# A recurrent network on one core: GpSimd's order in the steps with the key unit's squares

## The chip, the core and the metric

The kernel runs on one core of a Trainium2 chip. The metric is the device time of one execution in microseconds (us); less is better. Five engines work in parallel, each through its own list of instructions in order: TensorE (PE, matrix products; PEld is its loading of weights), VectorE (DVE), ScalarE (ACT), GpSimd (POOL) and SyncE (SP, which issues transfers). They wait for one another by semaphores.

## The reference

Two levels, each with an attention or state part and a feed-forward part, and at the end a gated sum. The input is 8 sequences of 512 tokens with 128 features. The change touches the last part only, a network of 6 layers:

```
x = level0(x)                       # linear attention, product-key memory
s = mixer_and_experts(norm(x))
for i in range(6):                  # the network
    x = attention(shift(x), Wqkv[i], q_scale[i], k_scale[i], Wo[i]) + x
    x = feed_forward(shift(x), ...) + x
out = x1 + s * silu(x)
```

Attention has 16 heads of 64. Queries and keys are divided by their norm (the root of the sum of their squares over the head), scaled and rotated; each token looks at itself and the 32 tokens before it; the softmax of the scores is taken and multiplied with the values.

## The kernel before

Levels 0 and 1 run first, up to about 2000 us, and are not touched. The network then runs as one software pipeline (function `network`). A **turn** is one layer of one sequence; 6 layers times 8 sequences make 48 turns. Most of them stand in a loop over layers (`Fori` in `turns`), the last ones behind it; one turn flows into the next without a barrier. A turn has 20 **steps**, numbered n. n divides into a group g = n // 5 of four heads and a window t = n % 5 of the tokens (the first of 128 queries, the others of 96, against 128 keys). The order of each engine is written out by hand: each has its own function `step(n, ...)`, and the order in which it calls its helpers is the order of its queue.

What runs in step n:

- PE: transposes the probabilities of step n-2 (`turn_probs`, L508, into the PSUM buffer c_S), scores of step n (`scores`, L493 adds the mask, L498 the products), values of step n-2 (`values`, L522).
- DVE: copies the transposed probabilities of step n-2 (`pt_copy`, L711), the reciprocal of the softmax sums of step n-1 (`inv_sum`, L704, writes c_rs), the row maxima of step n (`row_max`, L695).
- ACT: the output of step n-2 (`out_copy`, L396), the exponentials of step n (`exp`, L385, writes the probabilities c_Pb).
- POOL: the normalisation of the probabilities of step n-1, a product with c_rs (`normalise`, L323).

Beside this, in each group, one **query unit** and one **key unit** of a later group are prepared: two projections into the PSUM buffers c_PA and c_PB (L467 to L469), the squares of both (`square`, L363, on ACT, writes c_sq), their sum c_sqs (`add_squares`, L329, on POOL), the sum over the head (`sumsq`, L474, on PE), logarithm and exponential for the inverse norm (`inverse_norm`, L368 and L370, on ACT), the products with the tables of the rotation (`products`, L674, on DVE, write c_tAB), their sum c_rot (`rotate`, L335, on POOL) and the end (`finish`, L685, on DVE), from which SP copies the unit to its place. The key unit's sum of squares, `sumsq` and rotation stand in the steps with t = 1 (n = 1, 6, 11, 16), the query unit's in those with t = 3 and t = 4.

In a step with t = 1 PE goes through: `turn_probs`, `scores`, `values`, `sumsq` of the key unit, a projection for the values into c_PA (L479 to L481), and in some of them an output or feed-forward product. ACT, behind `exp` of the step, takes L368 and L370 and then copies that projection out of c_PA (`v_copy`, L374). What PE next writes into c_PA waits for this copy: a projection at the start of steps 2 and 17 (L479), the variance of the feed-forward part in step 7 (L541), the next query unit in step 12. `finish_turn` (L741, on DVE, in step 17) writes the new layer input.

Of the kernel before, what the change touches and what calls it, by code (L numbers as in the profile page):

```python
# [98 lines left out]
def network(nc, xf, wh_dram, wt_dram, tab_dram, const, depth, seqs):  # L99
# [8 lines left out]
    with ExitStack() as ctx:  # L108
# [104 lines left out]
        def query(t):  # L213
            return (0, TILE) if t == 0 else (LOOK + t * SPAN_Q, SPAN_Q)
# [4 lines left out]
        def job_k(g, now, nxt):  # L219
            return 2 * ((g + 1) % GROUPS) + 1, now if g < 3 else nxt  # L220

        def job_q(g, now, nxt):
            return 2 * ((g + 2) % GROUPS), now if g < 2 else nxt

        def back(n, d, now, prev):

            return (n - d, now) if n >= d else (n - d + NS, prev)
# [3 lines left out]
        def turns(eng, step):  # L231

            def one(now, nxt, prev, new=None, fresh=False):
                for n in range(NS):
                    step(n, now, nxt, prev, new, fresh)

            def at(l, s):
                return Turn(l, s, seqs)

            for n in range(12, NS):  # L240
                step(n, None, at(0, 0), None, None, False)
            one(at(0, 0), at(0, 1), None)
            with eng.Fori(0, depth - 1) as l:
                for s in range(1, seqs - 1):
                    one(at(l, s), at(l, s + 1), at(l, s - 1))
                one(at(l, seqs - 1), at(l + 1, 0), at(l, seqs - 2), new=l + 1)
                one(at(l + 1, 0), at(l + 1, 1), at(l, seqs - 1), fresh=True)
            l = depth - 1
            for s in range(1, seqs):
                one(at(l, s), at(l, s + 1) if s + 1 < seqs else None, at(l, s - 1))  # L250
            for n in range(18):
                step(n, None, None, at(l, seqs - 1), None, False)

        with nc.Block() as block:
# [59 lines left out]
            @block.gpsimd  # L314
            def _(pool):
                nc.gpsimd.memset(x1s[:, 0:1], 0.0).then_inc(*zeroed.up())

                def normalise(n, turn):
                    pool.wait_ge(*rs_ready.nth(n + 1, turn))
                    m = query(n % TIMES)[1]  # L320
                    p = Pb[0:m, n % 3]
                    r = rs[0:m, n % 2, :].unsqueeze(2).broadcast_to([m, 4, SPAN_K])
                    nc.gpsimd.tensor_tensor(p, p, r, ALU.mult).then_inc(*p_ready.up())  # L323

                def add_squares(j, turn):
                    pool.wait_ge(*squared.nth(2 * j + 2, turn))
                    if j or not turn.first:
                        pool.wait_ge(*summed.nth(j, turn))
                    nc.gpsimd.tensor_tensor(sqs[:, :], sq[:, 0], sq[:, 1], ALU.add).then_inc(*added.up())  # L329

                def rotate(j, turn):
                    pool.wait_ge(*prods.nth(2 * j + 2, turn))
                    if j or not turn.first:
                        pool.wait_ge(*finished.nth(j, turn))
                    nc.gpsimd.tensor_tensor(rot[:, :, :], tAB[:, 0], tAB[:, 1], ALU.add).then_inc(*rotated.up())  # L335

                def step(n, now, nxt, prev, new, fresh):
                    g, t = divmod(n, TIMES)
                    jk, tk = job_k(g, now, nxt)
                    jq, tq = job_q(g, now, nxt)  # L340
                    m, tm = back(n, 1, now, prev)
                    if t == 1 and tk:
                        add_squares(jk, tk)
                    if tm:
                        normalise(m, tm)
                    if t == 1 and tk:
                        rotate(jk, tk)
                    if t == 3 and tq:
                        add_squares(jq, tq)
                    if t == 4 and tq:  # L350
                        rotate(jq, tq)

                turns(pool, step)

            @block.scalar
# [1531 lines left out]
```

## Time and profile before

| what | before |
|---|---|
| median of three runs | 6846.82 us (6841.19 to 6852.91) |
| the profiled execution: time, span of its trace | 6850.26 us, 6848.5 us |
| PE busy | 5618.6 us (82% of the span) |
| DVE busy | 4308.3 us (63%) |
| ACT busy | 3758.7 us (55%) |
| POOL busy | 2607.8 us (38%) |
| the two GpSimd operations that change places | L323: 960 times, mean 1037 ns; L329: 384 times, mean 1268 ns |

The span is that of the trace of one execution. A busy share is a mean over stages with different limits; where time is lost is read in the timeline: a row gives the start, the length, the engine, the source line and the operation, and in brackets how long the engine had been idle and whose work released it. The network fills the span from about 2000 us to its end.

### The profile page before, as it was taken

Reading aid. Unit: us, or ns where it says so; the run is one execution under the profiler, and the core shown is the slowest. Engines: PE = TensorE matmul, PEld = TensorE weight load, DVE = VectorE, ACT = ScalarE, POOL = GpSimd, SP = SyncE. Lnnn points to the kernel's source line nnn. Section 1 sums busy time; section 2 is a strip of 40 time slices with the busy share of each in tenths; the row PEclk is TensorE's granted clock in tenths of the full one; section 3 lists DMA queues with packets and bytes.
Section 4 is the critical chain, followed back from the end, with each engine's and each line's share of the span. In section 5 each row is a group of like instructions: output and inputs, shape, how many; then the busy total and the mean of one; then the engine's idle time right before and its main releaser. Section 6 shows DMA issues by size and latency. Waiting matters only on the chain. (4 is left out here: it accounts for less than half of the span.)

```text
span 6848.5 us, 104092 instructions
## 1 busy us (share of the span) xinstructions
PE 5618.6 (82%) x31008; PEld 3140.3 (46%) x31008; DVE 4308.3 (63%) x6894; ACT 3758.7 (55%) x11846; POOL 2607.8 (38%) x2011
## 2 busy tenths in 40 slices
PE   6777767677768888888888888888888888888887
PEld 2333333222225555555555555555555555555553
DVE  5677766333346666766676666766667666766664
ACT  3444333233226666666666666666666666666665
POOL 1122211000015454444444445454544444454452
PEclk9888888777769999999999999999999999999998
DMA  0000000000012112211122111211122111221112
GB/s 35 0 0 0 0 0 0 19 0 0 0 59 47 44 44 49 51 46 42 43 53 50 42 44 44 54 47 44 44 49 52 44 43 43 53 50 43 42 43 62
DMA packets 160223, 244.35 MB, mean 36 GB/s; under 512 B 51280, under 2 KB 51280, under 8 KB 158928
## 3 DMA queue, kind: packets, MB, share of 16 engines
q1 hardware_dynamic: 159696, 238.08, 14.2%
q8 instruction: 239, 3.92, 0.3%
q14 instruction: 288, 2.36, 0.1%
HBM read 30.26 MB, written 6.29 MB: 5 GB/s over the span
## 5 line engine op out<-in xcount | busy, mean ns | idle before, releaser
L323 POOL TENSOR_TENSOR c_Pb<-c_Pb,c_rs 96x512 f32<-96x512 f32 (+1 forms) x960 | 995.8, 1037 | 1593.7 <-DVE c_rs L704 1590.0
L385 ACT ACTIVATE c_Pb<-c_S,c_nb 96x128 f32<-96x128 f32 (+1 forms) x3840 | 1347.5, 360 | 107.3 <-DVE c_nb L695 102.2
L711 DVE COPY c_PTs<-c_S 128x384 f32<-128x384 f32 (+1 forms) x960 | 559.3, 583 | 953.6 <-PE c_S L508 951.2
L396 ACT ACTIVATE c_OT<-c_PO 128x192 f32<-128x192 f32 (+1 forms) x960 | 327.6, 341 | 1462.8 <-PE c_PO L522 1459.9
L335 POOL TENSOR_TENSOR c_rot<-c_tAB 128x1024 f32<-128x1024 f32 x384 | 909.9, 2369 | 1.2 <-DVE c_tAB L674 0.8
L695 DVE TENSOR_REDUCE c_nb<-c_S 96x4 f32<-96x512 f32 (+1 forms) x960 | 656.7, 684 | 381.8 <-PE c_S L498 373.4
L329 POOL TENSOR_TENSOR c_sqs<-c_sq 128x512 f32<-128x512 f32 x384 | 487.1, 1268 | 847.6 <-ACT c_sq L363 841.9
L385 ACT ACTIVATION_READ_ACCUMULATOR c_Pb<-c_S,c_nb 96x1 f32 (+1 forms) x3840 | 761.2, 198 | 0.0
L498 PE MATMUL c_S<-c_QK 64*96 64x128 f32 (+1 forms) x7680 | 683.9, 298 | 0.0
L508 PEld LDWEIGHTS c_S<-c,c_Pb 96*128 96x128 f32 (+1 forms) x3840 | 441.8, 141 | 445.9 <-issue 418.4
L493 PE MATMUL c_S<-c 128*96 128x256 bf16 (+1 forms) x1920 | 397.8, 290 | 252.0 <-DVE c_PTs L711 247.9
L522 PE MATMUL c_PO<-c_PTs,c_V 128*64 128x96 f32 (+1 forms) x7680 | 568.5, 271 | 1.3 <-DVE c_PTs L711 1.3
L498 PEld LDWEIGHTS c_S<-c_QK 64*96 64x96 f32 (+1 forms) x7680 | 475.7, 170 | 190.7 <-issue 190.7
L508 PE MATMUL c_S<-c,c_Pb 96*128 96x96 f32 (+1 forms) x3840 | 497.8, 251 | 9.1 <-issue 9.1
L979 POOL TENSOR_TENSOR a_AT<-a_AT,c 128x256 f32<-128x256 f32 x128 | 112.6, 880 | 903.7 <-ACT a_AT L1037 903.4
L522 PEld LDWEIGHTS c_PO<-c_PTs,c_V 128*64 128x64 f32 x7680 | 371.6, 140 | 142.4 <-issue 13.5
L493 PEld LDWEIGHTS c_S<-c 128*96 128x96 bf16 (+1 forms) x1920 | 177.7, 120 | 531.4 <-DVE c_PTs L711 442.1
L1122 PE MATMUL a_B<-a_AT,a_V 128*32 128x512 f32 (+3 forms) x1024 | 332.0, 472 | 80.8 <-POOL a_AT L980 80.8
L532 PE MATMUL c_PC<-c_OT,c_WT 128*128 128x512 f32 x768 | 386.6, 606 | 0.0
L685 DVE SCALAR_TENSOR_TENSOR c_F<-c_PA,c_rot 128x1024 f32<-128x1024 f32 x192 | 232.6, 1211 | 71.7 <-ACT c_PA L370 67.4
L467 PE MATMUL c_PA<-c_xh,c_WH 128*128 128x512 f32 x384 | 195.5, 509 | 96.6 <-DVE c_F L685 67.2
L363 ACT ACTIVATE c_sq<-c_PB 128x512 f32<-128x512 f32 x384 | 227.2, 592 | 72.3 <-PE c_PB L469 70.3
(264 smaller groups left out, 10760.1 us busy)
## 6 DMA issues: line engine op xcount, KB each, us to landing
c_QK<-c_F SPq DMA_DIRECT2D x3072, 64.0 KB, 2.0
c_stage<-in_w_heads SPq DMA_DIRECT2D x36, 256.0 KB, 3.0
c_WT<-in_w_tails SPq DMA_DIRECT2D x6, 537.5 KB, 4.5
b_W<-in_w_level SPq DMA_DIRECT2D x1, 3133.0 KB, 10.3
a_W<-in_w_level SPq DMA_DIRECT2D x1, 3078.0 KB, 10.4
c_WT<-in_w_tails SPq DMA_DIRECT2D x6, 512.0 KB, 3.7
x<-in_x SPq DMA_DIRECT2D x1, 2048.0 KB, 7.7
x_kept<-x SPq DMA_DIRECT2D x1, 2048.0 KB, 6.3
```

Of the source, the lines that this page charges most:

```text
L323: nc.gpsimd.tensor_tensor(p, p, r, ALU.mult).then_inc(*p_ready.up())
L329: nc.gpsimd.tensor_tensor(sqs[:, :], sq[:, 0], sq[:, 1], ALU.add).then_inc(*added.up())
L335: nc.gpsimd.tensor_tensor(rot[:, :, :], tAB[:, 0], tAB[:, 1], ALU.add).then_inc(*rotated.up())
L385: e = nc.scalar.activation(Pb[0:m, n % 3, i, :], S[0:m, 2 * (n % 2) + r, c * SPAN_K:(c + 1) * SPAN_K], ACT.Exp, bias=nb[0:m, n % 2, i:i + ...
L493: nc.tensor.matmul(S[0:m, 2 * (n % 2) + r, 0:2 * SPAN_K], const.identb[:, 0:m], const.mask[t > 0], start=True, stop=False, skip_group_chec ...
L498: mm = nc.tensor.matmul(S[0:m, 2 * (n % 2) + r, c * SPAN_K:(c + 1) * SPAN_K], QK[rows, g % 2, 0, c, q0:q0 + m], QK[rows, g % 2, 1, c, k0:k ...
L508: mm = nc.tensor.transpose(S[:, 2 * (n % 2) + r, to:to + m], Pb[0:m, n % 3, 2 * r + c, :], ident[0:m, 0:m])
L522: mm = nc.tensor.matmul(PO[64 * r:64 * r + 64, c * TILE:c * TILE + m], V[:, t, h * DH:(h + 1) * DH], PTs[:, n % 2, 2 * r + c, 0:m], start= ...
L532: nc.tensor.matmul(PC[:, :], WT[:, T_O + p * P:T_O + (p + 1) * P], OT[:, p, :], start=p == 0, stop=p == PAIRS - 1, skip_group_check=True). ...
L695: nc.vector.tensor_reduce(nb[0:m, n % 2].rearrange("p (b c) -> p b c", b=2), S[0:m, b:b + 2, 0:2 * SPAN_K].rearrange("p b (c k) -> p b c k ...
L711: nc.vector.tensor_copy(PTs[:, n % 2].rearrange("p (b c) q -> p b c q", b=2)[:, :, :, 0:m], S[:, b:b + 2, 2 * SPAN_K:].rearrange("p b (c q ...
L1122: mm = nc.tensor.matmul(B[32 * j:32 * j + 32, 6 + g % 2, i * TILE:SEQ], V[:, i, h, :], AT[:, h % 2, SPAN[i]:SPAN[i] + SEQ - i * TILE], sta ...
```

## The change

In GpSimd's `step`, `normalise` now stands ahead of the key unit's `add_squares`. The query unit's half of the function stays. Semaphores, instructions and the other engines' orders are the same.

```diff
                     m, tm = back(n, 1, now, prev)
+                    if tm:
+                        normalise(m, tm)
                     if t == 1 and tk:
                         add_squares(jk, tk)
-                    if tm:
-                        normalise(m, tm)
                     if t == 1 and tk:
                         rotate(jk, tk)
```

GpSimd's queue over a part of a turn, before; the second to fourth rows are one step with t = 1; c_sqs is the sum of squares, c_Pb the probabilities, c_rot the rotated unit:

```order
L323 TENSOR_TENSOR c_Pb<-c_Pb,c_rs 96x512
L329 TENSOR_TENSOR c_sqs<-c_sq 128x512
L323 TENSOR_TENSOR c_Pb<-c_Pb,c_rs 128x512
L335 TENSOR_TENSOR c_rot<-c_tAB 128x1024
L323 TENSOR_TENSOR c_Pb<-c_Pb,c_rs 96x512 x2
```

The same part now:

```order
L323 TENSOR_TENSOR c_Pb<-c_Pb,c_rs 96x512
L323 TENSOR_TENSOR c_Pb<-c_Pb,c_rs 128x512
L329 TENSOR_TENSOR c_sqs<-c_sq 128x512
L335 TENSOR_TENSOR c_rot<-c_tAB 128x1024
L323 TENSOR_TENSOR c_Pb<-c_Pb,c_rs 96x512 x2
```

The normalisation of the window with 128 queries has moved ahead of the key unit's sum of squares; the rotation behind both keeps its place, as do the normalisations behind it.

PE's queue at such a step, before and now: it takes the sum of squares (L474), the projection for the values (L479 to L481), and only then the transposes of the probabilities (L508):

```order
L474 MATMUL c_PB<-c_sqs,c 128x512
L479 MATMUL c_PA<-c_WH,c_xh 128x512
L480 MATMUL c_PA<-c_WL,c_xh 128x512
L481 MATMUL c_PA<-c_WH,c_xl 128x512
L508 MATMUL c_S<-c,c_Pb 128x128 x4
```

Nothing moves on PE, so both of GpSimd's results are asked for in the order sum of squares, then probabilities.

## Rows read from the trace of the kernel before

**Rows 1.** The waits of PE from 2100 to 6800 us: us in total, times, longest us.
```profile
PE c_S L493 <- DVE c_PTs L711: 242.6, 349, 2.7
PE c_PA L541 <- ACT c_V L374: 72.0, 47, 1.6
PE c_PA L479 <- ACT c_V L374: 59.2, 94, 1.6
```

**Rows 2.** One source line, L474: times that PE waited for GpSimd's sum.
```profile
  POOL c_sqs L329: 11.2, 10
```

**Rows 3.** One source line, L323: who waited for the normalised probabilities.
```profile
  PEld c_S L508: 0.4, 1
```

**Rows 4.** The timeline of step 1 of a turn; start us, us, engine, line, [idle before].
```profile
4516.83 1.28 POOL L329 TENSOR_TENSOR c_sqs<-c_sq 128x512 f32<-128x512 f32 x1 [3.13 <-ACT c_sq L363]
4516.85 0.17 DVE L704 RECIPROCAL c_rs<-c_sums 128x4 f32<-128x4 f32 x1
4518.06 1.04 POOL L323 TENSOR_TENSOR c_Pb<-c_Pb,c_rs 128x512 f32<-128x512 f32 x1
4518.42 1.13 PE L474 MATMUL c_PB<-c_sqs,c 128*128 128x512 f32 x2
4520.17 0.68 ACT L368 ACTIVATE c_lnr<-c_PB,c 128x512 f32<-128x512 f32 x1
4520.94 0.60 PE L508 MATMUL c_S<-c,c_Pb 128*128 128x128 f32 x4
4522.14 0.50 PE L479 MATMUL c_PA<-c_WH,c_xh 128*128 128x512 f32 x1 [0.60 <-ACT c_V L374]
```

**Rows 5.** The timeline early in the network, where PE waited for GpSimd's sum.
```profile
2032.72 1.26 POOL L329 TENSOR_TENSOR c_sqs<-c_sq 128x512 f32<-128x512 f32 x1 [6.44 <-ACT c_sq L363]
2034.04 1.12 PE L474 MATMUL c_PB<-c_sqs,c 128*128 128x512 f32 x2 [2.17 <-POOL c_sqs L329]
```

**Rows 6.** The timeline of step 6 of the same turn.
```profile
4542.15 1.13 PE L474 MATMUL c_PB<-c_sqs,c 128*128 128x512 f32 x2
4545.95 1.12 PE L541 MATMUL c_PA<-c_csq,c 128*128 128x512 f32 x2 [1.53 <-ACT c_V L374]
```

**Rows 7.** The timeline of step 11 and the start of step 12.
```profile
4564.12 0.17 DVE L704 RECIPROCAL c_rs<-c_sums 128x4 f32<-128x4 f32 x1
4565.70 1.13 PE L474 MATMUL c_PB<-c_sqs,c 128*128 128x512 f32 x2
4567.99 0.69 DVE L711 COPY c_PTs<-c_S 128x512 f32<-128x512 f32 x1 [1.97 <-PE c_S L508]
4568.74 0.42 PE L493 MATMUL c_S<-c 128*96 128x256 bf16 x2 [0.78 <-DVE c_PTs L711]
```

**Rows 8.** The timeline of step 16 and of step 17 behind it.
```profile
4592.52 0.17 DVE L704 RECIPROCAL c_rs<-c_sums 128x4 f32<-128x4 f32 x1
4594.10 1.12 PE L474 MATMUL c_PB<-c_sqs,c 128*128 128x512 f32 x2
4597.25 0.69 DVE L711 COPY c_PTs<-c_S 128x512 f32<-128x512 f32 x1 [2.83 <-PE c_S L508]
4597.86 0.16 DVE L704 RECIPROCAL c_rs<-c_sums 96x4 f32<-96x4 f32 x1
4597.94 1.50 DVE L741 SCALAR_TENSOR_TENSOR xf<-c_PC,c_WT,c_x1s 64x512 f32<-64x512 f32 x2
4598.10 1.04 POOL L323 TENSOR_TENSOR c_Pb<-c_Pb,c_rs 96x512 f32<-96x512 f32 x1 [1.80 <-DVE c_rs L704]
4599.48 0.69 DVE L690 COPY c_V<-c_PA 128x512 f32<-128x512 f32 x1
4600.09 0.68 DVE L695 TENSOR_REDUCE c_nb<-c_S 96x4 f32<-96x512 f32 x1
```

**Rows 9.** PE's longest wait in the turn, just at the low-clock stretch.
```profile
4579.21 0.79 PE L479 MATMUL c_PB<-c_WH,c_xh 128*128 128x512 f32 x1 [2.07 <-DVE c_tAB L674]
```

**Rows 10.** A window: us, busy us of each engine, PEclk, DMA share, GB/s.
```profile
4578.50:4585.20 6.70, 5.99 (x24) 3.61 (x25) 3.24 (x6) 2.71 (x15) 4.17 (x3) 0.50 0.00 0
```

## The prediction

> **What bounds the kernel now.** I read the page first, for the shares: PE is busy for 82% of the span, no engine for all of it, so the time is set by chains between engines, and what the change is worth must be read at the places where PE waits. The second view is the list of PE's waits in the network. The reader is to see there that PE waits most for the copied transposes of the probabilities and, with 72.0 and 59.2 us, for ScalarE's copy out of the buffer c_PA [rows 1]. The third is the two source lines that matter. GpSimd's sum of squares made its PE instruction wait 10 times in all, 11.2 us [rows 2], and GpSimd's normalised probabilities were waited for once, 0.4 us [rows 3]. Both results are in time before: a change of their order has nothing to take away, and it can only use up the slack of the one that now comes later. The fourth is the timeline of the steps with t = 1, at n = 1, 6, 11 and 16, for that slack.
>
> **What the change moves.** Nothing is added or removed. In 192 steps (4 in each of 48 turns) the normalisation (1.04 us) goes ahead of the sum of squares (1.28 us) [rows 4].
>
> The normalisation comes earlier. In step 1 it ends at 4518.06 + 1.04 = 4519.10; PE takes the transposes at 4520.94 [rows 4], 1.8 us later, since it has the sum over the head and a projection ahead of them in its queue. Nobody gets anything from it: 0.
>
> The sum of squares comes later, for two reasons: it stands behind 1.04 us of work, and that work waits for the reciprocal of DVE. In step 1 the reciprocal ends at 4516.85 + 0.17 = 4517.02 [rows 4]. GpSimd starts 0.08 us after such an end (reciprocal to 4598.02, normalisation from 4598.10) [rows 8]; the next GpSimd instruction starts 0.05 us before the end of its predecessor (4516.83 + 1.28 against 4518.06) [rows 4]; and PE starts 0.06 us after the sum's end where it waits for it (2032.72 + 1.26 against 2034.04) [rows 5]. So L474 can start 0.08 + 1.04 - 0.05 + 1.28 + 0.06 = 2.41 us after the end of the reciprocal: 4519.43 in step 1, where it started at 4518.42 [rows 4], 1.0 us later. In step 11 the same is 4564.29 + 2.41 = 4566.70 against 4565.70 [rows 7], 1.0 us; in step 16 it is 4592.69 + 2.41 = 4595.10 against 4594.10 [rows 8], 1.0 us. That it is the same each time is no chance: L474 follows the copy of the transposes through scores and values on PE, the reciprocal follows the same copy on DVE. I take 0.99 us, as the start-to-end times of the three are rounded up here.
>
> Scores and values of the step are ahead of L474 in PE's queue, so row maxima and exponentials of this step do not move. What is behind L474 does. How much of the 0.99 us reaches the next step differs:
>
> - Step 1. L474 ended at 4518.42 + 1.13 = 4519.55, and ACT took the logarithm at 4520.17, when its exponentials were done [rows 4]: 0.62 us of slack, of which I leave 0.06 to the handing over, as measured from GpSimd to PE. So logarithm, exponential and the copy out of c_PA come 0.99 - 0.56 = 0.43 us later. PE waited 0.60 us for that copy at 4522.14 [rows 4]; its own delayed transposes (4520.94 + 0.60 + 0.99 = 4522.53) end just before 4522.14 + 0.43 = 4522.57. The step hands on 0.43 us.
> - Step 6. PE waited 1.53 us at L541 for the same copy [rows 6], which is more than 0.99; again only ACT's 0.43 us arrives.
> - Step 11. Nothing asks for c_PA at once. The transposes come 0.99 us later, their copy too (4567.99), and the next scores waited 0.78 us for just this copy [rows 7]. All of the 0.99 us goes on.
> - Step 16. PE's projection behind the copy out of c_PA would come 0.43 us later, as in step 1. But on DVE the copy of the transposes (4597.25), the reciprocal, the new layer input (4597.94 + 1.50), the copy for the values (4599.48) and the row maxima (4600.09) stand back to back [rows 8]. They all move with the transposes, and with them the exponentials of step 17: 0.99 us.
>
> Per turn 0.43 + 0.43 + 0.99 + 0.99 = 2.84 us; times 48 that is 136 us. Nothing behind these places runs by a clock of its own, so a delay that reaches scores, row maxima and exponentials stays. Bounds: if only ACT's part came through everywhere, 192 x 0.43 = 83 us; if all came through everywhere, 192 x 0.99 = 190 us. Below zero is excluded for this term as long as L474 waits for the sum. The rotation's sum starts later too, by 0.2 us in step 1 and 1.0 us in step 16, and finds cover: its user is one step on, behind the row maxima.
>
> **The granted clock.** Each turn has one stretch at half clock (the level of 1.2 GHz) near the feed-forward's gelu: PEclk 0.50 over 6.70 us with PE busy 5.99 us of it [rows 10], beginning about where PE waited 2.07 us [rows 9]. At the full level this work would take 3.0 us less, so 3.0 us is the most that such a stretch costs. The change puts a new idle time of about 1 us into four other steps. The Trainium skill ("TensorE: Matmul & The Clock Gate", section "Why this matters for your kernels") warns of unbroken idle gaps of PE between bursts. By that rule the new waits, shorter than any gap it speaks of, cost no clock, and the sum stays 136 us; this trace agrees only in part, since its clock falls at a wait of 2.07 us, also shorter than those gaps. If in place of this one new half-speed stretch came with each turn, the sum would be 136 + 48 x 3.0 = 280 us. I take none, but keep it as a rival.
>
> **The sum.** 136 us on the profiled execution's 6850.26 us gives 6986; that execution stands 3.4 us above the median of the runs, so by the median it is 6846.8 + 136 = 6983 us, 2.0% slower.
>
> **The rivals.**
>
> 1. More than the full delay: new stretches at half clock in the steps with t = 1. For it: the new wait comes some 1.5 us behind the one for the copied transposes that many steps already have [rows 1]. Against: the steps keep PE busy before and behind. Over 6846.8 + 190 = 7037 us, up to 6846.8 + 280 = 7127.
> 2. Less than ACT's part: the delay is caught up in a wait that lies later (PE's 242.6 us for the copied transposes [rows 1] are such waits), or one turn's half-speed stretch falls on less work. For it: the waits are many. Against: what they wait for hangs on the delayed work itself. At 30 us, say, 6877; up to 6846.8 + 83 = 6930.
> 3. Faster: the normalised probabilities are what the steps really wait for, and the records of PE's queue hide it. The normalisation would end 2.27 us behind the old start of the sum in the kernel before and 0.19 + 0.08 + 1.04 = 1.31 us behind it now, about 1.0 us earlier, and that is worth at most 192 x 1.0 = 192 us, so 6655. It decides only where PE reaches L508 within 1.0 us of the end of the normalisation; in step 1 it is 1.8 us late, with the old order, and would be 3.8 us late now. One wait of 0.4 us [rows 3] speaks against it.
> 4. No change: PE is held behind `values` by something else for 1 us in all four steps. Rows 2 and the even 1.0 us speak against it; it would give 6847.
>
> **Chances.** The forecast (83 to 190 us more) 0.72; rival 1 0.11; rival 2 0.11, of which 0.02 below 14 us; rival 3 0.03; rival 4 0.03. 0.2%, or 14 us, is what a measurement of this kernel can tell from no change. So faster 0.03, same 0.05, slower 0.92. The range leaves out about a tenth on each side: the lower end is a little under ACT's part alone (6930), 6915; the upper is the full delay with a half-speed stretch in some turns (23 us more), 7060.
>
> **What would show it.** In the changed kernel's waits of PE a row L474 <- POOL c_sqs L329 must appear with some 190 waits of about 1 us. The wait of L479 for the copy out of c_PA must fall from 0.60 us to nearly nothing in step 1, and L541's from 1.53 by about 0.6 us. ACT must show a new wait before L368 of about 0.4 us. A turn must be about 2.8 us longer. The sum of the normalisation's waiters stays at nothing. Wrong would be: no wait at L474, a second half-clock stretch in the turns, or steps 11 and 16 that hand on no more than steps 1 and 6.

## The result, and the profile after

The changed kernel takes 7037.2 us (median of 4 runs, 7036.3 to 7047.3) where the kernel before took 6844.0 us beside it: a ratio of 1.0284, 95% interval 1.0266 to 1.0301, or 193 us more. The forecast was 6983 us, slower, in a range of 6915 to 7060. The direction and the place came as forecast; the size was 136 us against 193, and the granted clock, which the forecast left out, has a part in the difference.

The waits of PE in the network, kernel after, from 2100 to 6950 us (us in total, times, longest us), answer to [rows 1]:

```profile
PE c_S L493 <- DVE c_PTs L711: 220.3, 335, 1.4
PE c_PB L474 <- POOL c_sqs L329: 186.5, 188, 1.2
PE c_PA L541 <- ACT c_V L374: 39.0, 41, 1.0
PE c_PA L467 <- DVE c_V L690: 27.9, 46, 0.6
```

A wait of PE for GpSimd's sum of squares stands where none was: 188 of the 192 places, 186.5 us. The wait of L479 for ScalarE's copy out of c_PA (59.2 us in [rows 1]) has gone from the list, and that of L541 has shrunk from 72.0 to 39.0. A new one is behind DVE's copy for the values (L690), 46 times: step 17, where DVE's chain is the later one. The line of the normalisation says what its earlier start brought; who waited for it, kernel after, is the same row as [rows 3]:

```profile
  PEld c_S L508: 0.4, 1
```

The timeline of step 1 in a turn of the last layer, which has no half-clock stretch in this kernel, answers to [rows 4]:

```profile
6591.48 0.17 DVE L704 RECIPROCAL c_rs<-c_sums 128x4 f32<-128x4 f32 x1
6591.73 1.04 POOL L323 TENSOR_TENSOR c_Pb<-c_Pb,c_rs 128x512 f32<-128x512 f32 x1 [3.33 <-DVE c_rs L704]
6592.72 1.27 POOL L329 TENSOR_TENSOR c_sqs<-c_sq 128x512 f32<-128x512 f32 x1
6594.04 1.13 PE L474 MATMUL c_PB<-c_sqs,c 128*128 128x512 f32 x2 [0.92 <-POOL c_sqs L329]
6595.21 0.69 ACT L368 ACTIVATE c_lnr<-c_PB,c 128x512 f32<-128x512 f32 x1 [0.29 <-PE c_PB L474]
6596.56 0.60 PE L508 MATMUL c_S<-c,c_Pb 128*128 128x128 f32 x4
6597.19 0.50 PE L479 MATMUL c_PA<-c_WH,c_xh 128*128 128x512 f32 x1
```

From the end of the reciprocal (6591.65) to L474 it is 2.39 us, where 2.41 was worked out. ScalarE now waits for the sum over the head at L368, as it did not in [rows 4] (0.29 us here; 188 times and 114.6 us in all, 0.61 us in the mean, where about 0.4 was foreseen), and PE takes L479 straight behind its transposes, as foreseen. Steps 6, 11 and 16 of that turn show the same, with PE's wait at 0.91, 0.91 and 0.92 us. In step 17 DVE's chain of [rows 8] has moved as one piece:

```profile
6671.78 0.69 DVE L711 COPY c_PTs<-c_S 128x512 f32<-128x512 f32 x1 [3.82 <-PE c_S L508]
6672.39 0.16 DVE L704 RECIPROCAL c_rs<-c_sums 96x4 f32<-96x4 f32 x1
6672.47 1.50 DVE L741 SCALAR_TENSOR_TENSOR xf<-c_PC,c_WT,c_x1s 64x512 f32<-64x512 f32 x2
6674.00 0.69 DVE L690 COPY c_V<-c_PA 128x512 f32<-128x512 f32 x1
6674.61 0.68 DVE L695 TENSOR_REDUCE c_nb<-c_S 96x4 f32<-96x512 f32 x1
```

What the forecast did not have is in the granted clock. In an ordinary turn of the middle layers the changed kernel has two half-clock stretches. Here are the timeline of PE and two windows (us, busy us of each engine, PEclk, DMA share, GB/s) of one turn, kernel after; they answer to [rows 9, 10]. It is the second turn of its layer, which has a third stretch in step 1; the turns in the middle of a layer have these two alone:

```profile
4689.67 0.50 PE L479 MATMUL c_PB<-c_WH,c_xh 128*128 128x512 f32 x1 [2.07 <-DVE c_tAB L674]
4701.94 0.42 PE L493 MATMUL c_S<-c 128*96 128x256 bf16 x2 [0.65 <-DVE c_PTs L711]
4704.45 1.66 PE L474 MATMUL c_PB<-c_sqs,c 128*128 128x512 f32 x2 [0.99 <-POOL c_sqs L329]
4705.12 1.42 PE L479 MATMUL c_PA<-c_WH,c_xh 128*128 128x512 f32 x1
```
```profile
4691.30:4694.60 3.30, 3.30 (x15) 1.65 (x12) 1.28 (x2) 1.87 (x10) 2.29 (x1) 0.50 0.00 0
4704.95:4708.25 3.30, 3.30 (x7) 1.90 (x6) 0.00 (x0) 2.18 (x5) 1.68 (x1) 0.50 0.00 0
```

The first is in the place of the old stretch, in step 13, and shorter. The second is new. It begins in step 16, within half a us of the end of PE's new wait of 0.99 us, which follows one of 0.65 us; PE's work behind it (L479, 1.42 us here, 0.79 at full clock in the last layer) runs at half speed.

To see where a turn has become longer I use the distance between the starts of the row maxima (L695) of successive steps, its median over 16 ordinary turns (four from the middle of each of the second to fifth layers), in us; a turn is the sum of 20 such steps (for e3 and e4, whose turns differ, the shortest and the longest). Each row comes from the one traced execution of its kernel. The runs below stand beside it:

| kernel | step 1 | step 6 | step 11 | steps 13 + 14 | step 16 | turn |
|---|---|---|---|---|---|---|
| before | 5.93 | 6.15 | 4.48 | 12.1 | 6.35 | 99.0 |
| after | 6.40 | 6.63 | 5.53 | 11.0 | 8.98 | 102.4 |
| e1, before, PE kept busy | 5.92 | 6.15 | 4.48 | 9.4 | 6.36 | 96.3 |
| e2, after, PE kept busy | 6.33 | 6.57 | 5.47 | 9.4 | 7.34 | 99.1 |
| e3, new order in 1 and 6 | 6.41 | 6.63 | 4.48 | 11.0 | 6.36 | 97.2 to 101.8 |
| e4, new order in 11 and 16 | 5.92 | 6.15 | 5.53 | 12.0 | 9.05 | 98.4 to 102.8 |
| e5, half the normalisation | 5.93 | 6.16 | 5.04 | 9.4 | 6.93 | 97.5 |
| e6, the wait alone | 5.92 | 6.15 | 4.70 | 9.4 | 6.57 | 96.7 |
| e7, after, busy in step 16 | 7.93 | 6.63 | 5.53 | 11.0 | 7.34 | 102.4 |

### The profile page after: what moved, and what is told of

The parts are those of the page before. It is cut to its first block and busy times, and to the rows that moved or that the text cites. A ratio compares the mean times of both kernels' runs of the same rounds, so it can differ in the third digit from the quotient of the medians.

```text
span 7036.3 us, 104092 instructions
## 1 busy us (share of the span) xinstructions
PE 5690.0 (81%) x31008; PEld 3162.1 (45%) x31008; DVE 4317.6 (61%) x6894; ACT 3779.3 (54%) x11846; POOL 2611.8 (37%) x2011
## 5 line engine op out<-in xcount | busy, mean ns | idle before, releaser
L323 POOL TENSOR_TENSOR c_Pb<-c_Pb,c_rs 96x512 f32<-96x512 f32 (+1 forms) x960 | 996.7, 1038 | 2410.6 <-DVE c_rs L704 2410.6
L695 DVE TENSOR_REDUCE c_nb<-c_S 96x4 f32<-96x512 f32 (+1 forms) x960 | 656.9, 684 | 333.9 <-PE c_S L498 326.7
L508 PEld LDWEIGHTS c_S<-c,c_Pb 96*128 96x128 f32 (+1 forms) x3840 | 449.6, 143 | 451.9 <-issue 425.0
L508 PE MATMUL c_S<-c,c_Pb 96*128 96x96 f32 (+1 forms) x3840 | 506.2, 254 | 9.4 <-issue 9.4
L474 PE MATMUL c_PB<-c_sqs,c 128*128 128x512 f32 x384 | 264.2, 776 | 193.4 <-POOL c_sqs L329 193.4
```

What stands on the lines that cost most here:

```text
L508: mm = nc.tensor.transpose(S[:, 2 * (n % 2) + r, to:to + m], Pb[0:m, n % 3, 2 * r + c, :], ident[0:m, 0:m])
L695: nc.vector.tensor_reduce(nb[0:m, n % 2].rearrange("p (b c) -> p b c", b=2), S[0:m, b:b + 2, 0:2 * SPAN_K].rearrange("p b (c k) -> p b c k ...
```

## The experiments

The theory, A: the new wait is 0.99 us in each of the 192 steps and hands on 2.8 us a turn at full clock; the rest of the 193 us is the granted clock, of which the new waits cost a second stretch. The first rival, B: the clock does not matter, and all of it is delay handed on.

**e1_before_busy and e2_after_busy: the clock taken out of the comparison.** In both, PE repeats products that it does anyway (a projection's first product in step 13, the transposes of step 14), inside waits of PE; the results stay the same. In e2 it also has small products in front of the sum.

```diff
+                        if n == 13:
+                            w = slice(H_QK + jq * 2 * P + P, H_QK + jq * 2 * P + 2 * P)
+                            for _ in range(4):
+                                nc.tensor.matmul(PB[:, :], WH[:, w], xh[:, tq.seq % 2], start=True, stop=True)
                         proj(jq, 1, tq, PB)
...
-                    for r in range(2):
+                    for r in tuple(range(2)) if n != 12 else 4 * tuple(range(2)):
...
+                    if n in (1, 6, 11, 16) and tk:                  # e2 only
+                        pe.wait_ge(*prods.nth(2 * jk + 1, tk))
+                        pe.wait_ge(*squared.nth(2 * jk + 1, tk))
+                        for _ in range(6):
+                            nc.tensor.matmul(PB[:, 0:256], const.identb, const.mask[0], start=True, stop=True)
```

> The kernel before, with PE given repeats of products it does anyway (4 of a projection in step 13, the four transposes of step 14 three times more), in waits of PE of 1.1 and 2.1 us that stand around the half-clock stretch of each turn; results unchanged. Theory A (the new wait hands on 2.8 us a turn at full clock, and the rest of the 193 us is the clock): the stretch goes, and a turn falls from 99.0 us by what it cost. The four turns of the changed kernel without any stretch take 98.9 us with 2.8 us of handed-on delay in them, so a turn without either should take 96.1 us and the run about 6844 - 47 x 2.9 = 6708 us. Theory B (the clock does not matter, all 193 us are handed-on delay): no gain, or up to 1 us a turn slower for the added products, 6844 to 6890 us.

> The changed kernel with the same repeats in steps 13 and 14, and six small bf16 products on PE (about 0.1 us each) inside the new 1 us wait ahead of the sum over the head, so that PE is busy there. Theory A: no half-clock stretch in most turns, 135 us (48 x 2.8) above the kernel before with the repeats, about 6843 us. Theory B: 193 us above the kernel before with the repeats.

Measured: e1 6755.3 us, 0.9866 of the kernel before (0.9850 to 0.9882); e2 6870.1 us, 1.0034 (1.0020 to 1.0048). Half-clock stretches are left in both, 13 in e1 and 9 in e2, most of them in the turns around a change of layer. One window of 100 us in each, e1 first, has the granted clock at its full level throughout:

```profile
4550.00:4650.00 100.00, 88.64 (x614) 55.13 (x612) 67.69 (x106) 64.72 (x230) 50.25 (x37) 1.00 0.19 43
```
```profile
4550.00:4650.00 100.00, 89.66 (x621) 55.50 (x620) 65.72 (x103) 64.08 (x228) 50.03 (x38) 1.00 0.19 43
```

Theory B is out: more work on PE made the kernel before faster by 92 us. The stretch's price stands in the table: steps 13 and 14 fall from 12.1 to 9.4 us, the turn from 99.0 to 96.3, 2.7 us. The expected 6708 us was missed: of 136 us 44 did not come, some 25 of them in the 15 turns around a change of layer (three at each of the five changes), which take 96 to 105 us in e1 and gained only about 1.2 us each. Between e1 and e2 the four steps grow by 0.41, 0.42, 0.99 and 0.98 us and nothing else does: 2.80 us a turn. The row maxima of steps 11 and 12, then 16 and 17, e1 and e2:

```profile
4521.74 0.69 DVE L699 TENSOR_REDUCE c_nb<-c_S 96x4 f32<-96x512 f32 x1
4526.23 0.69 DVE L699 TENSOR_REDUCE c_nb<-c_S 96x4 f32<-96x512 f32 x1 [1.05 <-PE c_S L498]
4547.38 0.69 DVE L699 TENSOR_REDUCE c_nb<-c_S 96x4 f32<-96x512 f32 x1
4553.73 0.68 DVE L699 TENSOR_REDUCE c_nb<-c_S 96x4 f32<-96x512 f32 x1
```
```profile
4582.95 0.69 DVE L704 TENSOR_REDUCE c_nb<-c_S 96x4 f32<-96x512 f32 x1
4588.42 0.69 DVE L704 TENSOR_REDUCE c_nb<-c_S 96x4 f32<-96x512 f32 x1 [1.05 <-PE c_S L498]
4609.58 0.69 DVE L704 TENSOR_REDUCE c_nb<-c_S 96x4 f32<-96x512 f32 x1
4616.92 0.68 DVE L704 TENSOR_REDUCE c_nb<-c_S 96x4 f32<-96x512 f32 x1
```

4.49 and 6.35 us have become 5.47 and 7.34. Over the whole run the new order costs 6870.1 - 6755.3 = 115 us, where 135 were expected, with the clock out of it in the ordinary turns.

**e3_first_in_1_and_6 and e4_first_in_11_and_16: one part of the change alone.**

```diff
+                    if n in (1, 6) and tm:                          # e4: (11, 16)
+                        normalise(m, tm)
                     if t == 1 and tk:
                         add_squares(jk, tk)
-                    if tm:
+                    if n not in (1, 6) and tm:
                         normalise(m, tm)
```

> The new order in steps 1 and 6 alone, the old one in 11 and 16. Theory A: ScalarE's slack takes 0.56 of the 0.99 us in these two steps, so 0.41 to 0.48 us each, 39 to 46 us in all, and no new half-clock stretch: 6883 to 6890 us. Theory B (each of the four steps hands on a quarter of the 193 us): 6940 us.

> The new order in steps 11 and 16 alone. Theory A: 0.99 us each, 95 us, and on top of it the second half-clock stretch that the changed kernel has in step 16 (up to 50 us): 6939 to 6990 us, and together with the run for steps 1 and 6 it makes up the whole 193 us. Theory B: 6940 us, with the same again for steps 1 and 6.

Measured: e3 6887.5 us, 1.0055 (1.0039 to 1.0072), 40 us more; e4 6974.2 us, 1.0187 (1.0170 to 1.0204), 126 us more. The halves are as unequal as theory A has them, and together make 166 of the 193 us; the whole, as e4's expectation had it, they do not make, and no run here tells where the other 27 are. In PE's waits, e3 first, each shows the wait of 1 us in half of the places, with the same total:

```profile
PE c_PB L476 <- POOL c_sqs L329: 93.3, 95, 1.2
```
```profile
PE c_PB L476 <- POOL c_sqs L329: 92.2, 93, 1.2
```

The same wait costs three times as much in steps 11 and 16, clock included (at full clock, in e2, 1.97 us a turn against 0.83). e4 has the new stretch in step 16 (9.05 us there) in 31 turns. Against the expectation e3 also has new ones, 24 of them in steps 1 and 6, where the kernel before has one; its turns vary between 97.2 and 101.8 us. That its time still lies in the expected 6883 to 6890 us is in part luck: steps 13 and 14 are 1.2 us shorter than before, since the stretch there has become shorter, and pay for the new ones.

**e5_half_normalise: the size of the work ahead of the sum.** This is e2 with half of the normalisation left out.

```diff
                     m = query(n % TIMES)[1]
-                    p = Pb[0:m, n % 3]
-                    r = rs[0:m, n % 2, :].unsqueeze(2).broadcast_to([m, 4, SPAN_K])
+                    heads = 2 if n % TIMES == 0 else 4
+                    p = Pb[0:m, n % 3, 0:heads]
+                    r = rs[0:m, n % 2, 0:heads].unsqueeze(2).broadcast_to([m, heads, SPAN_K])
```

> The new order with PE kept busy as in e2_after_busy, but the normalisation that stands ahead of the sum of squares does only two of its four heads (in every group's first window the other two stay unnormalised), so it should take some 0.5 us instead of 1.04. Theory A (what costs is the work ahead of the sum, less a fixed slack of 0.56 us on ScalarE in steps 1 and 6): PE's wait for the sum falls from 0.99 to about 0.47 us; steps 1 and 6 then hand on nothing, steps 11 and 16 hand on 0.47 us each: a turn at 96.3 + 0.94 = 97.2 us, and the run 48 x 1.87 = 90 us under e2_after_busy, about 6780 us. Rival C (each step's loss is in proportion to the wait): all four halve, 97.7 us a turn, 6803 us. Rival D (the place in the queue costs, not the length): as e2_after_busy, 6870 us.

Measured: 6791.1 us, 0.9927 (0.9910 to 0.9943). The timeline of step 11 in e5:

```profile
4536.60 0.61 POOL L324 TENSOR_TENSOR c_Pb<-c_Pb,c_rs 128x256 f32<-128x256 f32 x1 [3.23 <-DVE c_rs L714]
4537.18 1.27 POOL L330 TENSOR_TENSOR c_sqs<-c_sq 128x512 f32<-128x512 f32 x1
4538.60 1.02 PE L475 MATMUL c_PB<-c_sqs,c 128*128 128x512 f32 x2
4539.68 0.68 ACT L369 ACTIVATE c_lnr<-c_PB,c 128x512 f32<-128x512 f32 x1
```

The half took 0.61 us, not 0.5, so the delay is 0.99 - 0.43 = 0.56 us. Steps 1 and 6 are back at 5.93 and 6.16 us, nothing handed on; steps 11 and 16 hand on 0.56 and 0.57 us. The turn is at 97.5 us, 1.2 over e1. This settles two things: the loss follows the length of the work ahead of the sum (rival D is out), and ScalarE's slack in steps 1 and 6 is a threshold, not a share (rival C is out): it takes up all of 0.56 us here and 0.99 - 0.41 = 0.58 us in e2.

**e6_wait_alone: the wait without the work.**

```diff
                     if t == 1 and tk:
+                        if tm:
+                            pool.wait_ge(*rs_ready.nth(m + 1, tm))
                         add_squares(jk, tk)
                     if tm:
                         normalise(m, tm)
```

> The old order with PE kept busy as in e1_before_busy; in front of the key unit's sum of squares GpSimd also waits for the reciprocal, whose product still comes behind the sum. So the sum meets the new wait without the 1.04 us of work. Theory A: the sum can be used 1.42 us after the reciprocal's end (0.08 + 1.28 + 0.06), which is 4518.44 in step 1, where PE took it at 4518.42: the wait alone costs at most 0.05 us a step, nothing is handed on, 6755 us as e1_before_busy (within 10 us). Rival E (the wait for the reciprocal is a part of the loss): up to 0.2 us a step handed on in steps 11 and 16, 6775 us.

Measured: 6767.3 us, 0.9892 (0.9876 to 0.9909); steps 11 and 16 are 0.22 and 0.21 us longer than in e1, steps 1 and 6 not at all. That is nearer to rival E's 6775 us than to theory A's 6755. The timeline of e6 shows what was missed, first around step 16 of a turn in the loop over layers, then around step 16 of a turn behind the loop:

```profile
4550.59 0.17 DVE L710 RECIPROCAL c_rs<-c_sums 128x4 f32<-128x4 f32 x1
4551.00 1.27 POOL L329 TENSOR_TENSOR c_sqs<-c_sq 128x512 f32<-128x512 f32 x1 [4.63 <-DVE c_rs L710]
4552.40 1.12 PE L476 MATMUL c_PB<-c_sqs,c 128*128 128x512 f32 x2 [0.15 <-POOL c_sqs L329]
```
```profile
6405.01 0.17 DVE L710 RECIPROCAL c_rs<-c_sums 128x4 f32<-128x4 f32 x1
6405.26 1.27 POOL L329 TENSOR_TENSOR c_sqs<-c_sq 128x512 f32<-128x512 f32 x1 [4.49 <-DVE c_rs L710]
6406.59 1.12 PE L476 MATMUL c_PB<-c_sqs,c 128*128 128x512 f32 x2
```

In the loop GpSimd begins the sum 0.24 us after the reciprocal's end, not 0.08, and PE begins L476 0.13 us after the sum's end, not 0.06: 1.64 us together, where 1.42 was reckoned, and the difference is the 0.22 us. Behind the loop both are as reckoned (0.08 and 0.06 us), and there steps 11 and 16 take 4.48 and 6.36 us as in e1: the wait alone costs nothing. The sum has three semaphore waits in front of it in this kernel and L476 has two; each one that is taken after the wait that lets go last costs about 0.08 us in the loop and none behind it. No experiment varied the number of waits by itself, and why the loop matters is open. In the changed kernel the sum's own waits pass while the normalisation runs. So of the 0.99 us the normalisation's own work is the part that counts, and the wait for the reciprocal would be nearly free if it were not for the further waits.

The same explains a small thing in the table. L474 of the changed kernel starts 0.13 us after the sum's end in the loop, where 0.06 was reckoned, and 0.05 us after it behind the loop; in e2, and in step 16 of e7, the small products in front of it have taken its second wait before, and it starts 0.05 us after the sum's end in the loop too. That is why steps 1, 6 and 11 are 0.06 to 0.07 us longer in the changed kernel than in e2; behind the loop they are as long as e2's.

**e7_busy_in_step_16: where the second stretch comes from.** The small products of e2, in step 16 of the changed kernel alone.

> The changed kernel, with the six small products in PE's wait for the sum in step 16 alone; steps 13 and 14 as they were, so the first half-clock stretch stays. Theory A (the second stretch, in step 16, is brought by the new wait there): it goes in most turns, step 16 falls from 9.0 to about 7.3 us, the first stretch takes back part of it (steps 13 and 14 up to 0.6 us longer, as in the kernel before with its longer stretch); a turn at 101.8 us, some 30 to 60 us under the changed kernel, 6980 to 7007 us. Theory F (the second stretch has nothing to do with the wait): 7037 us.

Measured: 6991.7 us, 1.0220 (1.0203 to 1.0237), 45 us under the changed kernel. Step 16 is at 7.34 us and has no stretch in any turn: without the idle time there is no stretch there, theory F is out. But an ordinary turn still takes 102.4 us, not the 101.8 expected, for in 27 turns a stretch now lies in step 1 (7.93 us), where the changed kernel has one in three. The 45 us come almost wholly from the 15 turns around a change of layer (38 us between the two traces). The timeline of PE and a window there, e7:

```profile
2330.90 0.42 PE L493 MATMUL c_S<-c 128*96 128x256 bf16 x2 [0.65 <-DVE c_PTs L716]
2333.39 2.07 PE L474 MATMUL c_PB<-c_sqs,c 128*128 128x512 f32 x2 [0.98 <-POOL c_sqs L329]
```
```profile
2333.40:2336.60 3.20, 3.20 (x6) 1.89 (x7) 0.00 (x0) 1.85 (x8) 2.16 (x1) 0.50 0.11 26
```

The pattern is that of step 16: a wait of 0.65 us for the copied transposes, 1.5 us of work, the new wait of about 1 us, and then half clock. Stretches come in steps 1, 6 and 16 in one kernel or another once these have both waits; in which of them differs from kernel to kernel.

Two short waits close together are not enough, though. In ordinary turns of the changed kernel the same pair stands in steps 1, 6 and 11 as well, 0.65 and 0.99 us each, at full clock. In a turn of the last layer it stands in all four steps, and PE's wait of 2.08 us in step 13 too, with no stretch anywhere. Step 16 of that turn in the changed kernel, two rows of PE and the window (PEclk 1.00):

```profile
6666.19 0.42 PE L493 MATMUL c_S<-c 128*96 128x256 bf16 x2 [0.65 <-DVE c_PTs L711]
6668.62 0.70 PE L474 MATMUL c_PB<-c_sqs,c 128*128 128x512 f32 x1 [0.92 <-POOL c_sqs L329]
```
```profile
6667.27:6674.61 7.34, 5.93 (x40) 3.52 (x40) 3.45 (x8) 4.01 (x13) 4.66 (x4) 1.00 0.08 18
```

What decides which of the pairs draws a stretch no run here varied.

**e8_before_busy_more: the best version.** e1, with the transposes also repeated in steps 11, 12 and 15 of the turns that prepare a new layer.

```diff
-                    for r in tuple(range(2)) if n != 12 else 4 * tuple(range(2)):
+                    for r in (4 if n == 12 or late and n in (9, 10, 13) else 1) * tuple(range(2)):
```

> The kernel before with the repeats of e1_before_busy, and the transposes of steps 11, 12 and 15 also taken four times in the turns that prepare a new layer, where that kernel still has half-clock stretches and PE waits up to 2.6 us for the copied transposes. Theory A: these stretches (10 of them, up to 1.7 us each) go, the repeats lie in the waits: 6738 to 6755 us. Otherwise, the repeats delay the copies there: 6755 to 6775 us.

Measured: 6747.7 us, 0.9866 of the kernel before (0.9850 to 0.9882). That is the ratio of e1 to the last digit, so the addition brings nothing that can be told; both are 1.3% faster than the kernel before.

## Why the prediction was right, and where its size was off

- *The place.* Right: the sum of squares is late for L474, in all 192 places, in 180 of them by 0.91 to 0.99 us and in ten, next to a change of layer, by 1.25. The chain 0.08 + 1.04 - 0.05 + 1.28 + 0.06 = 2.41 us came out at 2.39 behind the loop and 2.47 in it.
- *The early normalisation brings nothing.* Right: its one wait of 0.4 us is the same before and after. Rivals 3 and 4 are out.
- *What each step hands on.* Forecast 0.43, 0.43, 0.99, 0.99; measured between e1 and e2 at full clock 0.41, 0.42, 0.99, 0.98. ScalarE's slack and DVE's chain in step 17 were read rightly; e5 shows the slack as a threshold. In the loop of the changed kernel, with L474's second wait, it is 0.06 to 0.07 us more in each.
- *Times 48.* A little too high, as far as e1 and e2 show. From the first to the last row maxima of the network, e2 is 121.8 us behind e1, not 136: 89.3 in the other turns, and 32.5 in the 15 turns around a change of layer, 2.2 us each and not 2.8. Two causes are possible and were not told apart: DVE prepares new weights there and PE waits for it, which can cover part of the delay; or the clock, for e1 has 41.0 us at half clock in these turns and e2 20.5, and by half of PE's busy time in them that alone could hide 10 us.
- *The granted clock.* This is the step that was mis-sized: "I take none". Between the same two places the changed kernel is 182.7 us behind the kernel before, 61 us more than the 121.8. Up to 12 of the 61 are no clock but L474's second wait (160 places in the loop, 0.075 us each); the other 50 or so go with the half-clock stretches. In ordinary turns little of it is lost: the half-clock work costs 1.5 us in steps 13 and 14 and 1.6 in step 16 (0.06 of which is the second wait), 3.2 in place of 2.7. Most, 54 of the 61, lies around a change of layer, where the loss is 86.5 us in 15 turns, 5.8 each, against 32.5 between e1 and e2. The clock records agree: in these 15 turns the time at half clock grows from 102.4 us before to 221.9 after, and in the others, the last six turns aside, it is 184.3 us in both kernels. As an estimate, half of PE's busy time in all stretches, which is how the prediction priced one, is 145 us before and 200 after, 55 more. In the last five full turns the changed kernel does no worse: it has no stretch and takes 98.9 us, as the kernel before does with its stretch; so the delay of 2.8 us was paid for there by the clock.
- The prediction had named "a second half-clock stretch in the turns" as a sign of being wrong, and this sign came. The measured time lies in the range because its upper end had 54 us of room for a delay handed on in full, which did not come, and 23 us for stretches, where some 50 came: the one room covered the other, which is luck.
- Rival 1 had the mechanism (new stretches in the steps with t = 1) at a chance of 0.11. The rows it rested on were right; its price was not, for the new stretches brought some 50 us, not up to 48 x 3.0 = 144, and the measured time stands at the very lower edge of its 7037 to 7127 us. The 3.0 us given as the most that one stretch costs holds: e1 gained 2.7. The rule of the Trainium skill ("TensorE: Matmul & The Clock Gate", "Why this matters for your kernels") that was weighed there speaks of one unbroken gap; e7 and the changed kernel show half clock behind two waits of 0.65 and 0.99 us with 1.5 us of work in between, so here the trace does not agree with it. That [rows 9] had already shown the clock to fall at a gap shorter than the rule's should have moved more of the chance.

The whole: 122 us of delay that is handed on, some 50 us of clock and some 10 us of L474's second wait make the 183 us of the network. The remaining 5 us of the two profiled executions' 188 lie ahead of its first row maxima; e1, with the old order there, has the same 5 us, so they are no part of the change.

## What to carry to other kernels

In a hand-ordered pipeline the slack of each of two results, against the instruction that takes it, says which goes first: here one had 1.8 us and the other 0.3, and 1 us of work was put before the wrong one. A delay is handed on only past what the next engine is still busy with, so the same 1 us wait cost 0.4 us in two places and 1.0 in two others; look for the chain that the delayed engine feeds, which need not be the one it waits for. And where PE shows half-clock stretches, look for short waits close together too, not only for a long one: taking away one of the pair took away the stretch (e7), though the same pair stood elsewhere at full clock. Products repeated inside PE's waits made the kernel 1.3% faster.

## What was not expected of the hardware

Repeating work on PE (four projection products and twelve transposes a turn) shortened every ordinary turn by 2.7 us. In the loop over layers each semaphore wait taken after the one that let go last put off an instruction by about 0.08 us, on GpSimd (0.24 us after the release with two such waits in e6, 0.08 with none) and on PE (0.13 against 0.05 us at L474); behind the loop the same waits cost nothing. In one place of each layer, step 11 of its second turn, e6 has 0.52 us, and in the turn ahead of the loop 0.41; no run tells why. Turns with quite different half-clock stretches (after: steps 13 and 16; e7: steps 1 and 13) settled at the same length of 102.4 us; no run here tells why.
